# First norm of a six-layer Perceiver kernel: rows loaded in four pieces, statistics for each, gamma and beta applied to the transposes; half of the first context's DMA issues in the next stage

## What is computed

```
x = x + bidirectional_attention(layernorm(x), ctx, w_sim, b_sim, W_qv, b_qv)
x = x + causal_attention(layernorm(x), ...)
x = x + mixture_of_experts(layernorm(x), ...)
x = x + cross_attention(layernorm(x), ctx, ctx, mask, ...)
x = x + differential_attention_block(layernorm(x), ...)
x = x + ternary_ffn(layernorm(x), ...)
```

## Time and profile before

| what | us |
|---|---|
| median of 3 runs | 2830.17 (2828.04 to 2832.3) |
| the profiled execution's own time | 2828.69 |
| its span in the trace | 2826.7 |
| TensorE busy in the span | 2628.9 (93%) |
| VectorE busy | 1752.5 (62%) |
| ScalarE busy | 1453.6 (51%) |
| GpSimd busy | 116.0 (4%) |
| DMA, mean over the span | 89 GB/s |

### The profile page before, as it was taken

One profiled execution on the slowest core, in us unless ns is written; L12 is line 12 of the kernel. 1 busy time (PEld: TensorE's weight loads), 2 busy tenths in 40 slices (PEclk: granted clock), 3 DMA queues, 4 the chain that ended last, 5 costly groups with the idle time before them and its releaser, 6 DMA issues. The chain is left out here.

```text
span 2826.7 us, 58825 instructions
## 1 busy us (share of the span) xinstructions
PE 2628.9 (93%) x24437; PEld 2055.8 (73%) x24440; DVE 1752.5 (62%) x4193; ACT 1453.6 (51%) x3010; POOL 116.0 (4%) x104
## 2 busy tenths in 40 slices
PE   6999899889979999999999999999999887789987
PEld 3444578679858788887888888887888676667764
DVE  4333532647665666667666667666666688764487
ACT  2111212336535666666666666666576524635774
POOL 0000200120020000000000000000000022010000
PEclk9999999999989999999999999999999988889988
DMA  7888201258751112101111011110111010114300
GB/s 256 304 298 306 71 1 49 88 204 275 250 158 48 41 50 50 43 20 38 50 50 48 15 38 50 49 48 15 38 50 40 32 64 2 40 64 145 124 11 30
DMA packets 204265, 250.99 MB, mean 89 GB/s; under 512 B 77777, under 2 KB 133073, under 8 KB 203745
## 3 DMA queue, kind: packets, MB, share of 16 engines
q1 hardware_dynamic: 194784, 222.07, 25.1%
q10 hardware_dynamic: 6656, 16.78, 1.8%
q0 software_dynamic: 2560, 8.39, 0.9%
HBM read 223.07 MB, written 24.12 MB: 87 GB/s over the span
## 5 line engine op out<-in xcount | busy, mean ns | idle before, releaser
L91 PE MATMUL xa_J<-xa_c_hi,xa_wk_hi 128*128 128x402 f32 x1024 | 360.0, 352 | 1.7 <-POOL xa_m L2558 1.7
L93 PE MATMUL xa_J<-xa_c_hi,xa_wk_lo 128*128 128x402 f32 x1024 | 354.7, 346 | 0.0
L92 PE MATMUL xa_J<-xa_c_lo,xa_wk_hi 128*128 128x402 f32 x1024 | 354.6, 346 | 0.0
L2315 ACT ACTIVATE xa_pr<-xa_pr,xa_ri 128x416 f32<-128x416 f32 x512 | 280.1, 630 | 141.5 <-DVE xa_ri L2443 141.5
L91 PE MATMUL xa_J<-xa_wv_hi,xa_c_hi 128*128 128x512 f32 (+1 forms) x832 | 338.9, 407 | 0.0
L92 PE MATMUL xa_J<-xa_wv_lo,xa_c_hi 128*128 128x512 f32 (+1 forms) x832 | 327.8, 394 | 0.0
L93 PE MATMUL xa_J<-xa_wv_hi,xa_c_lo 128*128 128x512 f32 (+1 forms) x832 | 326.8, 393 | 0.0
L2305 ACT ACTIVATE xa_pr<-xa_pr,xa_local 128x416 f32<-128x416 f32 x512 | 321.5, 632 | 0.0
L2292 ACT ACTIVATE xa_kT<-xa_J,cl_bk 128x402 f32<-128x402 f32 x256 | 151.2, 591 | 329.0 <-PE xa_J L93 323.3
L2417 DVE CUSTOM_DVE_ANT_0 xa_pr<-xa_S,xa_m 128x416 f32<-128x416 f32 x512 | 271.7, 587 | 23.2 <-PE xa_S L2603 22.2
L2455 DVE TENSOR_TENSOR cl_v<-xa_J,main_x 128x512 f32<-128x512 f32 (+1 forms) x208 | 143.4, 689 | 221.4 <-PE xa_J L93 193.7
(11 more groups left out here) (519 smaller groups left out, 5030.5 us busy)
## 6 DMA issues: line engine op xcount, KB each, us to landing
bl_rows<-in_ctx SPq DMA_DIRECT2D x40, 1024.0 KB, 8.9
main_x<-in_ctx_cols SPq DMA_DIRECT2D x192, 201.0 KB, 3.3
bl_cols<-in_ctx_cols SPq DMA_DIRECT2D x24, 1024.0 KB, 10.7
moe_raw<-in_L_ffn_routed_w SPq DMA_DIRECT2D x45, 512.0 KB, 5.0
main_qoT<-in_L_ffn_w ACTq DMA_DIRECT2D x32, 512.0 KB, 3.8
main_x<-in_ctx_cols SPq DMA_DIRECT2D x64, 197.5 KB, 3.3
main_qoT<-in_L_attn_W SPq DMA_DIRECT2D x16, 512.0 KB, 3.6
routed_in<-main_qoT SPq DMA_DIRECT2D x1, 7680.0 KB, 22.5
```

Of the source, the lines that this page charges most:

```text
L91: pe.matmul(out, w_hi, x_hi, start=first, stop=False)
L92: pe.matmul(out, w_hi, x_lo, start=False, stop=False)
L93: return pe.matmul(out, w_lo, x_hi, start=False, stop=last)
L2315: nc.scalar.activation(now, now, ACT.Copy, scale=ri[:, i:i + 1]).then_inc(scaled, 1)
```

## The change

- `start_stage` no longer loads x; only GpSimd's identity is left in it.
- `norm_stage` is replaced by `first_norm_stage`. SP issues x in four pieces of two tiles with a semaphore each, then gamma and beta as columns (`g_col`, `b_col`, 128 partitions x 4 values, 1,024 single values in all), then `prefetch`. VectorE waits for a piece ahead of its two `bn_stats`.
- h is written to `hc` once, even tiles by ScalarE and odd tiles by VectorE. TensorE transposes h itself, into all eight PSUM banks, one half of the tokens at a time with a bank for each chunk. gamma and beta are applied while a half leaves PSUM, as scale and bias for each partition: chunks 0 and 1 by ScalarE, chunks 2 and 3 by VectorE, each over 512 columns. The buffer `hcw` is gone.
- `load_pair` ends after the last `load_cols`. What followed is `load_pair_end` (the next pair's `early` rows and the first batch's rows, 4.1 MB), which SP issues at the head of `bidaf_scores_stage`.

```diff
@@ first_norm_stage (in place of norm_stage), SP
+                for i in range(PIECES):
+                    ts = slice(i * each, (i + 1) * each)
+                    sp.dma_start(x_sb[:, ts, :], rows_in[:, ts, :]).then_inc(x_loaded[i], 16)
+                with nc.allow_non_contiguous_dma(reason="1024 values, once"):
+                    sp.dma_start(g_col[:], gamma.rearrange("(k p) -> p k", p=P)).then_inc(affine_loaded, 16)
+                    sp.dma_start(b_col[:], beta.rearrange("(k p) -> p k", p=P)).then_inc(affine_loaded, 16)
+                prefetch(sp)
@@ VectorE
                 for t in range(TILES):
+                    if t % each == 0:
+                        dve.wait_ge(x_loaded[t // each], 16)
                     last = nc.vector.bn_stats(stats[:, t, :], x_sb[:, t, :])
...
-                for t in range(TILES):
...
-                    nc.vector.scalar_tensor_tensor(y[:, t, :], x_sb[:, t, :], mv[:, t, 0:1], g_sb[:], ALU.subtract, ALU.mult).then_inc(mid, 1)
-                    dve.wait_ge(mid, t + 1)
-                    nc.vector.scalar_tensor_tensor(y[:, t, :], y[:, t, :], rstd[:, t:t + 1], b_sb[:], ALU.mult, ALU.add).then_inc(normed, 1)
...
+                for t in range(1, TILES, 2):
+                    nc.vector.tensor_scalar(xn[:, t, :], x_sb[:, t, :], mv[:, t, 0:1], rstd[:, t:t + 1],
+                                            ALU.subtract, ALU.mult).then_inc(xn_dve, 1)
+                dve.wait_ge(affine_loaded, 32)
+                for h in range(HALVES):
+                    dve.wait_ge(turned_ready, h + 1)
+                    for k in range(KC // 2, KC):
+                        nc.vector.tensor_scalar(affine_out(h, k), turned[:, h, k, :], g_col[:, k:k + 1], b_col[:, k:k + 1], ALU.mult, ALU.add)
@@ ScalarE
+                for t in range(0, TILES, 2):
+                    nc.scalar.activation(xn[:, t, :], x_sb[:, t, :], ACT.Identity, bias=shift[:, t:t + 1], scale=rstd[:, t:t + 1])\
+                        .then_inc(xn_act, 1)
+                act.wait_ge(affine_loaded, 32)
+                for h in range(HALVES):
+                    act.wait_ge(turned_ready, h + 1)
+                    for k in range(KC // 2):
+                        nc.scalar.activation(affine_out(h, k), turned[:, h, k, :], ACT.Identity, bias=b_col[:, k:k + 1], scale=g_col[:, k:k + 1])
@@ TensorE
+                for t in range(TILES):
+                    if t % 2 == 0:
+                        pe.wait_ge(xn_act, t // 2 + 1)
+                    else:
+                        pe.wait_ge(xn_dve, t // 2 + 1)
+                    for k in range(KC):
+                        last = pe.transpose(turned[:, t // GROUP, k, (t % GROUP) * P:(t % GROUP + 1) * P], xn[:, t, k * P:(k + 1) * P], ident[:])
+                    if t % GROUP == GROUP - 1:
                         last.then_inc(turned_ready, 1)
@@ PairLoads.load_pair
         for g in range(GROUPS):
             self.load_second(sp, 0, g)
             self.load_cols(sp, 0, g)
+
+    def load_pair_end(self, sp):
         self.load_early(sp, 1)
         for g in range(GROUPS):
             self.load_first(sp, 0, g)
@@ bidaf_scores_stage, SP
             def _(sp):
+                loads.load_pair_end(sp)
                 for t in range(TILES):
@@ start_stage
-            @block.sync
-            def _(sp):
-                sp.dma_start(x_sb[:], x.rearrange("(t a) s d -> (a s) t d", a=2)).then_inc(x_loaded, 16)
-                sp.wait_ge(x_loaded, 16)
```

More of the change, by code:

```diff
@@ L117, in unused_semaphores, with first_norm_stage @@
     return runs
-def norm_stage(nc, stage, x_sb, xn, ident, gamma=None, beta=None, y=None, yT=None, hi=None, lo=None,
-               prefetch=None, clear=False):
+def first_norm_stage(nc, stage, x, x_sb, xn, ident, gamma, beta, yT, prefetch):
+    GROUP, PIECES = 4, 4
     with ExitStack() as ctx:
@@ L129, in norm_stage, with affine_out @@
         table = s.sb("table", [P, 1])
[L130 to L144, removed]
+        ve, sd, r0, r1, r2, rstd, shift = (s.sb(n, [P, TILES]) for n in ("ve", "sd", "r0", "r1", "r2", "rstd", "shift"))
+        g_col, b_col = s.sb("gamma", [P, KC]), s.sb("beta", [P, KC])
+        turned = s.ps("turned", [P, HALVES, KC, HALF])
+        x_loaded = [s.sem(f"x_loaded{i}") for i in range(PIECES)]
+        affine_loaded, chain, var_ready, sd_ready, shift_ready = (s.sem(n) for n in (
+            "affine_loaded", "chain", "var_ready", "sd_ready", "shift_ready"))
+        xn_act, xn_dve, turned_ready = s.sem("xn_act"), s.sem("xn_dve"), s.sem("turned_ready")
+        rows_in = x.rearrange("(t a) s d -> (a s) t d", a=2)
+        each = TILES // PIECES
+        def affine_out(h, k):
+            return yT[:, k, h * HALF:(h + 1) * HALF]
         with nc.Block() as block:
@@ L185, in _ @@
                 link(nc.vector.tensor_tensor(rstd[:], r0[:], r1[:], ALU.mult))
-                if gamma is not None:
-                    nc.vector.scalar_tensor_tensor(shift[:], mv[:, :, 0], -1.0, rstd[:], ALU.mult, ALU.mult).then_inc(shift_ready, 1)
-                    dve.wait_ge(affine_loaded, 32)
-                for t in range(TILES):
[L190 to L193, removed]
-                    nc.vector.scalar_tensor_tensor(y[:, t, :], x_sb[:, t, :], mv[:, t, 0:1], g_sb[:], ALU.subtract, ALU.mult).then_inc(mid, 1)
-                    dve.wait_ge(mid, t + 1)
-                    nc.vector.scalar_tensor_tensor(y[:, t, :], y[:, t, :], rstd[:, t:t + 1], b_sb[:], ALU.mult, ALU.add).then_inc(normed, 1)
[L197 to L201, removed]
+                nc.vector.scalar_tensor_tensor(shift[:], mv[:, :, 0], -1.0, rstd[:], ALU.mult, ALU.mult).then_inc(shift_ready, 1)
+                for t in range(1, TILES, 2):
[6 more added lines that the diff above has]
+                        nc.vector.tensor_scalar(affine_out(h, k), turned[:, h, k, :], g_col[:, k:k + 1], b_col[:, k:k + 1], ALU.mult, ALU.add)
             @block.scalar
@@ L207, in _ @@
                 nc.scalar.activation(sd[:], ve[:], ACT.Sqrt).then_inc(sd_ready, 1)
[L208 to L217, removed]
+                act.wait_ge(shift_ready, 1)
+                for t in range(0, TILES, 2):
[6 more added lines that the diff above has]
+                        nc.scalar.activation(affine_out(h, k), turned[:, h, k, :], ACT.Identity, bias=b_col[:, k:k + 1], scale=g_col[:, k:k + 1])
             @block.tensor
             def _(pe):
[L221 to L227, removed]
-                        for k in range(KC):
-                            last = pe.transpose(turned[:, t % 4, k * P:(k + 1) * P], src[:, t, k * P:(k + 1) * P], ident[:])
+                for t in range(TILES):
[6 more added lines that the diff above has]
+                    if t % GROUP == GROUP - 1:
                         last.then_inc(turned_ready, 1)
@@ L932, with context_layers @@
 TOKEN_GROUPS = [(0, 4), (4, TILES)]
-def context_layers(nc, x_sb, ident, ctx_rows, ctx_cols, w_sim, b_sim, W, bias, Wq, bq, Wk, bk, Wv, bv, Wo, bo,
+def context_layers(nc, x, x_sb, ident, ctx_rows, ctx_cols, w_sim, b_sim, W, bias, Wq, bq, Wk, bk, Wv, bv, Wo, bo,
                    late, experts):
```

13 lines of the change are left out of this document (5 added, 8 removed).

## The result

Six runs of the changed kernel have a median of 2,815.45 us (2,810.61 to 2,821.51), six of the kernel before 2,829.76. The ratio is 0.9952, 95% interval 0.9941 to 0.9962: 13.6 us less, between 10.8 and 16.7. Five more runs beside eleven of before gave 0.9950 (0.9937 to 0.9964). The profiled execution took 2,816.83, with a span of 2,815.1 where that of before was 2,826.7.

The account below looks back on a forecast made before the run. The prediction took the first norm's block to end with SP's DMA issues, 4.62 us after its arithmetic. Starting the scores stage at 21.3 instead of 35.36 gains 14.1 us: 2,830.17 becomes 2,816.1, range from a gain of 16 plus 2.7 spread to 2,822.

Parts of the forecast that it names:

- Part 1: Loading x inside the norm stage: stage begins at 1.91 instead of 9.55, statistics end at 11.1 instead of 14.44.
- Part 2: Scaling, transposes and affine in the norm: arithmetic ends at 20.0 us instead of 30.20.
- Part 3: Gamma and beta column loads: 1,024 four-byte packets take 0.56 us of the DMA queue.
- Part 4: Half of the first context's issues leave the norm stage: SP done at 20.8, scores stage starts at 21.3.
- early bound 19.5: Byte-count check on when SP finishes issuing in the norm stage, earlier than the 20.8 kept.
- Part 5: Moved issues at the head of the scores stage's SP queue end by about 31 and cost nothing.
- The sum: Scores stage starts at 21.3 instead of 35.36, a gain of 14.1 us, bounds 12.5 to 16.
- shifted by one constant: All stages after the scores stage's earlier start were to move by the same amount.
- SP as the bound: Rival: another issue stall in the norm stage leaves SP done at 24.8; gain 10.1, time 2,820.1; chance 0.10.
- The pieces overlap: Rival denied this: x's pieces load in turn, scores stage starts at 26.9; gain 8.4, time 2,821.8; chance 0.04.
- The four-byte loads didn't clog the queue: Rival said they would: at 0.35 us per packet the kernel is 7.7 us slower, 2,837.9; chance 0.03.
- The scores stage didn't lose its pace: Rival said it would: five tiles taking the long form lose 7.8 us of gain, time 2,823.9; chance 0.09.

Follow-up runs that it names:

- x in one piece: The changed kernel with x loaded by one DMA instead of four; scores stage starts at 26.95 us, ratio to the kernel before 0.9955.
- x alone moved: The kernel before with only x's load moved into the norm stage in four pieces; scores stage starts at 33.60 us, ratio 0.9981.
- the pair whole: The changed kernel with SP again issuing the whole first pair in the norm stage; scores stage starts at 32.29 us, ratio to the kernel before 0.9976.
- the new body alone: The kernel before with only the new norm body, x loaded in the start stage and the pair unsplit; scores stage starts at 33.94, ratio 0.9989.

## Why the prediction was right, and where it was not

The forecast was 2,816.1 and the result 2,815.45; the range held. Step by step:

- **Part 1**, begin of the stage: forecast 1.91, measured 1.85. Arrival of x: forecast 9.9, measured 11.07 at the latest (10.7 to 11.5 over the profiles), and 10.8 with the queue to itself. I applied 370 GB/s throughout, and the load in pieces has a gap. Term off by about 1 us; that the statistics hide under the load was right, and x in one piece showed the price of not doing so.
- **Part 2**, the largest miss: arithmetic ended at 23.82, not 20.0. Of the 3.8 us, 1.3 come from the late statistics. The rest is the rate of the transposes: I took the price of a warm run (0.5 us for four) for an engine that had waited 15.6 us. They ended 4.55 us after ScalarE's last scaled tile (22.24 against 17.69), where 1.6 had been allowed. The trace of before already had the hint, 1.11 us for four in the earlier trace rows and 2.79 for the twelve at 35.36. With TensorE kept busy the 32 took 3.66. An eviction alone cost 0.77 and 0.81, where I had 0.69 and 0.75, but two that follow each other took 1.45 and 1.53, which is what the sum had (1.5). VectorE's scaling at its lower bound (0.48) changed nothing, as said.
- **Part 3**: the column loads cost nothing that could be measured; no engine waited for them. SP's last column issue of the pair ended at 21.68 with the broadcast loads (x alone moved) and at 19.96 with the four-byte ones; the 0.52 MB saved are 1.3 us of these 1.7. The 0.56 us of part 3 are not seen.
- **Part 4**: SP done at 19.96, between my early bound 19.5 and the 20.8 I kept. Counting what is ahead in the queue also gave the three other kernels' last issues (31.3 forecast and 31.74 measured with the pair whole, 32.6 and 33.05 with x alone, 34.1 and 33.40 with the new body alone). The arithmetic and the issues were called equal; in fact the arithmetic ended 3.9 us later. The split was still worth 8.2 us of start.
- **Part 5**: SP was ready for the next pair at 31.3, ahead of the release at 32.05; in a later profile it was not quite (31.59 against a reduction at 30.92), and nobody waited for it. TensorE waited for no row or column of the first pair.
- **The sum**: a start 2.8 us later than forecast, and TensorE's level paid 1.7 us of it back, since it was slow in the norm but came fast into the scores stage: the first reduction is 7.93 us into the stage, not 9.6. Forecast 30.9 for it, measured 32.05 and 30.92; a lead of 13.0 and 14.1 where 14.1 was forecast. The agreement of the totals is better than the steps deserve. Two errors of opposite sign, most of the first and all of the second from one overlooked state, nearly cancel; then the lead grew by 2.4 us up to the merge stage in one profile and lost 0.3 in the other, and 7.4 and 6.0 us of it went in the middle of the kernel, which the forecast had as shifted by one constant. That 2,816.1 met 2,815.45 so closely is luck: the interval of the gain alone runs from 10.8 to 16.7 us.
- **Rivals**: SP as the bound fell (19.96 against 23.82). The pieces overlap. The four-byte loads didn't clog the queue. The scores stage didn't lose its pace, it waited 2.2 us less in one profile (7.4 against 9.6 us on both kinds of load); that is not the change's doing, since its second profile waited 9.5 us.

What stays open: why the stretch from 408 to 833 us is longer in the profiles of the whole change and its variants (418.1 to 426.1 us against 417.5 to 418.4), in stages that the change does not touch; and the gap in the load of x. The 3 us that the lead wins back by the end (8.5 to 11.6) are within the scatter of the last stretch, which took 1,979.3 to 1,985.5 us over all thirteen profiles.

## What to carry to other kernels

A stage that ends with all its queues ends with the slowest of them, the one that only issues DMAs included; find which ends last before pricing any arithmetic in it, because each part alone brought 1.3 to 5.5 us here and the whole 13 to 14. When work is moved to another place in the program, price matmuls and transposes by rows where TensorE ran at the level that it will have there, and read that level from the count in a microsecond: a transpose took up to 0.23 us at the slow level and 0.11 to 0.125 in a busy stretch. The idle time just ahead does not settle it, as 2.79 us for twelve after a pause of 0.94 us shows; the work before the pause counts too. And where runs scatter by 5 us, follow an early event (the next stage's start) in the profiles rather than the total, and then check at a few later events that the lead is still there.

## What the runs showed of the hardware that I had not expected

- TensorE's slow level is worth 1.5 to 3.0 us on 32 transposes (5.14 to 6.62 against 3.66) and 1.29 us on twelve (2.79 against 1.50). It came after 15.6 us and 5.8 us of idleness, but also after 0.94 us behind sparse work. The granted clock column gave 1.00 for both levels in the first 22 us of the kernel after and the first 40 of the kernel before.
- The load of x in four DMAs dropped to 113 to 256 GB/s between 6 and 7 us in all nine profiles that have it (231 and 160 in the two of after, 172 with x moved alone, 199 with nothing behind it), with and without other loads behind it; as one DMA the queue moved 377 GB/s there, and yet the load was complete hardly earlier (10.75).
- An issue stalls by what is outstanding in packets, it seems, and not in bytes. With x as one DMA (1,024 packets of 2 KB) and the two column loads (1,024 of four bytes) ahead of it, SP's next issue took 3.71 us, at 3.52; in the kernel before, the first long one (4.02 us, at 14.10) had 5.0 MB issued and 0.8 MB moved ahead of it, by estimate about 2,000 packets of 2 KB outstanding. In bytes the two differ by a factor of two. No run was made to test this.
